# A graph network kernel on one core: the fourth sorted step of the third pass gathered by GpSimd instead of selected by TensorE

## The reference

```
h = relu(layernorm(x));                  # L0: two GCN convolutions
    h = relu(segment_sum((h @ W1)[src] * norm, dst) + b1)     # pass 1
    h = segment_sum((h @ W2)[src] * norm, dst) + b2           # pass 2
x = x + log_softmax(h)
h = relu(layernorm(x));                  # L1: GIN with edge attributes
    msg  = relu(h[src] + edge_attr @ We + be)                 # pass 3
    aggr = segment_sum(msg, dst)
    y = relu((h + aggr) @ W1 + b1) @ W2 + b2
x = x + relu(batchnorm(y) * gamma + beta)
```

## Time and profile before

| | us |
|---|---|
| median of 3 runs | 5606.34 |
| lowest, highest | 5599.08, 5607.18 |
| the profiled execution | 5616.2 |
| its span, first to last instruction | 5614.4 |
| TensorE busy, share of the span | 77% |
| GpSimd busy | 67% |
| VectorE busy | 66% |
| ScalarE busy | 23% |
| mean granted TensorE clock | 0.855 |

### The profile page before, as it was taken

The page is one execution under the profiler, slowest core; times in us unless marked ns, Lnnn a source line. Parts: engine busy times, 40 slices in busy tenths (PEclk is TensorE's granted clock), DMA queues, the critical chain, the costliest instruction groups (busy, mean ns, idle before and its releaser), DMA issues.

```text
span 5614.4 us, 116632 instructions
## 1 busy us (share of the span) xinstructions
PE 4328.9 (77%) x29893; PEld 3358.6 (60%) x29894; DVE 3689.5 (66%) x10748; ACT 1292.0 (23%) x4287; POOL 3768.6 (67%) x3554
## 2 busy tenths in 40 slices
PE   4566666666666666668999999996699999999995
PEld 4444444444444444456777777775577777777773
DVE  3466666665666666647888888886666666666662
ACT  5111111111111111142111111113433333332223
POOL 2377777777777777737777777775666665666663
PEclk6577787777778787859999999996899999999997
DMA  2122222222222222212222222223232322222224
GB/s 54 37 47 46 50 47 47 48 47 48 46 48 46 49 48 49 46 52 52 52 51 51 51 51 51 51 48 111 65 70 65 70 68 66 70 62 67 63 59 109
DMA packets 239972, 316.92 MB, mean 56 GB/s; under 512 B 69263, under 2 KB 175178, under 8 KB 239545
## 3 DMA queue, kind: packets, MB, share of 16 engines
q0 software_dynamic: 111232, 170.85, 15.6%
q1 hardware_dynamic: 128688, 145.48, 8.9%
HBM read 276.92 MB, written 39.15 MB: 56 GB/s over the span
## 4 chain that ended last, share of the span: by engine, by line
PE 60%; DVE 13%; POOL 11%; issue 10%; DVEq 2%; ACT 2%; DMA 1%; POOLq 0%; ACTq 0%; SPq 0%
PE psum L1222 26%; PE psum L1142 15%; POOL rows_g L658 11%; PE psum L1165 7%; PE psum L1129 3%; DVE x_tab L1662 2%; PE psum L1086 2%; PE psum L1150 2%; PE psum L1154 1%; DVE x_tab L1657 1%; DVEq L432 1%; PE psum L1214 1%; PE psum L1289 1%; DMA rows_g<-table,idx 1%; DVE rows_g L1619 1%
## 5 line engine op out<-in xcount | busy, mean ns | idle before, releaser
L658 POOL DMA_INDIRECT rows_g<-table,idx x3476 | 3605.6, 1037 | 1547.3 <-issue 1011.3
L1222 PE MATMUL psum<-x_tab 125*128 x8512 | 1148.9, 289 | 83.9 <-issue 46.2
L1142 PE MATMUL psum<-hot,rows_g 128*96 128x128 f32 x7512 | 1077.4, 297 | 143.5 <-DMA rows_g<-table,idx 70.7
L1142 PEld LDWEIGHTS psum<-hot,rows_g 128*96 128x96 f32 x7512 | 980.8, 181 | 236.4 <-issue 145.8
L1222 PEld LDWEIGHTS psum<-x_tab 125*128 125x128 bf16 x8512 | 827.3, 97 | 393.9 <-issue 135.0
L1165 PE MATMUL psum<-x_tab 128*104 128x512 bf16 x2432 | 614.5, 403 | 534.4 <-DVE x_tab L1662 526.3
L1582 DVE TENSOR_TENSOR acc<-acc,psum 96x128 f32 x1173 | 328.8, 280 | 962.9 <-PE psum L1142 945.2
L791 ACT ACTIVATE attr<-edge 128x12 f32 (+1 forms) x1173 | 243.5, 211 | 2806.3 <-PE psum L1142 2805.6
L1165 PEld LDWEIGHTS psum<-x_tab 128*104 128x104 bf16 x2432 | 303.1, 133 | 780.6 <-ACT x_tab L848 321.9
L1573 DVE TENSOR_SCALAR hot<-iota,attr 128x128 f32<-128x128 f32 x2504 | 686.4, 356 | 7.3 <-ACT acc L785 4.8
L1619 DVE TENSOR_REDUCE rows_g<-psum 128x384 f32<-128x1152 f32 x304 | 412.3, 1356 | 341.2 <-PE psum L1222 336.9
(11 more groups left out here) (255 smaller groups left out, 3692.3 us busy)
## 6 DMA issues: line engine op xcount, KB each, us to landing
rows_g<-table,idx POOLq DMA_INDIRECT x3476, 2.5
x_tab<-sorted_keys SPq DMA_DIRECT2D x304, 125.0 KB
x_more<-in_edge_attr_dram SPq DMA_DIRECT2D x238, 64.0 KB
sorted_attr<-x_tab SPq DMA_DIRECT2D x38, 384.0 KB
x_more<-sorted_attr SPq DMA_DIRECT2D x152, 96.0 KB
table<-x_tab SPq DMA_DIRECT2D x13, 840.0 KB
x_tab<-in_edge_attr_dram SPq DMA_DIRECT2D x38, 256.0 KB, 2.8
x_tab<-in_x_dram SPq DMA_DIRECT2D x2, 4200.0 KB
```

The source lines that it names most:

```text
L658: pool.indirect_dma_start(out=rows_g[u][0:np_, g * F:(g + 1) * F], out_offset=None, in_=table[p], in_offset=bass.IndirectOffsetOnAxis(ap=i ...
L1142: last = pe.matmul(ps_agg[t.b], rows_g[t.u][0:t.np_, g * F:(g + 1) * F], hot[t.h][0:t.np_, g, :], start=g == 0, stop=g == G - 1)
L1222: last = pe.matmul(ps_sel[c], mask[i % 2][j][:, c * P:(c + 1) * P], tab3[:, j:J - KB + 1 + j, :, :][:, bass.ds(w[c], 1), :, :].rearrange(" ...
```

## The change

In pass 3 the fourth sorted step of each iteration (step 9, `SEL[3]`, `MIX = 3`) is fetched by GpSimd like a gathered step: 4 indirect DMAs more per iteration. Its 40 selecting matmuls and its 10 masks go. Its edge term is still made by the four matmuls of L1214 from the sorted attributes, as a sum of three parts; `join_rows` adds up the parts into a scratch tile `terms` (which lies over mask tiles that nobody uses then), waits for itself and for the gather, and adds `terms` to the gathered rows. The key of that step is still loaded and converted. The mask semaphore is raised without masks.

Since the fourth select now has no masks, the transposes and products of the edge attributes that stood between them move: `EA_AT` now has two in stretch 1 (at masks 2 and 6), one in stretch 2 (at mask 4) and none in stretch 3. VectorE's edge terms follow (`TERMS`: 3, 2, 1, 0 per stretch instead of 3, 1, 1, 1), ScalarE's copies too (`COPY_AT`, `COPY_PAST`), and SyncE's loads of attributes are spread as 1, 1, 2, 2 over the stretches instead of 3, 2, 1, 0, with the first three ahead of the loop.

```diff
@@ Step
             def selected(self, p):
-                return p > 0 and self.sel
+                return p > 0 and self.sel and not self.mixed(p)
+            def mixed(self, p):
+                return p == 2 and self.sel and self.i == MIX
...
@@ SyncE, load_iter
-                    for k in ((0, 1, 2), (3, 4), (5,), ())[i]:
-                        t = Gather(it, k)
-                        load_ea(fast, t.gi, t.s, t.h, EP)
+                    for k in ((3,), (4,), (5, 6), (7, 8))[i]:
+                        t = Gather(it + k // NG, k % NG)
+                        load_ea(fast, t.gi, t.s, t.h, t.np_)
...
@@ ScalarE, gin_iter
+            COPY_AT, COPY_PAST = {0: (0,), 1: (1,), 2: (2,), 4: (3,), 5: (5,)}, {4: (4,)}
...
                     for k in SEGS[i]:
-                        if k in GAT:
-                            gin_copy(Gather(it, GAT.index(k) + LL))
+                        for g in COPY_AT.get(k, ()):
+                            gin_copy(Gather(it, g + LL))
                         relu_fast(Step(it, k))
+                        for g in COPY_PAST.get(k, ()):
+                            gin_copy(Gather(it, g + LL))
...
@@ TensorE, select
-                w = starts(it, i)
+                w = None if p == 2 and i == MIX else starts(it, i)
...
+                mixed = p == 2 and i == MIX
...
-                for j in range(KB):
+                for j in range(0 if mixed else KB):
...
-            EA_AT = ({2: 0, 5: 1, 8: 2}, {5: 3}, {5: 4}, {5: 5})
+            EA_AT = ({2: 0, 5: 1, 8: 2}, {2: 3, 6: 4}, {4: 5}, {})
...
@@ VectorE, make_masks
+                if p == 2 and i == MIX:
+                    dve.sem_inc(s_mask, KB)
+                    return
...
@@ VectorE, join_rows
+                if t.mixed(p):
+                    dve.tensor_reduce(terms.rearrange("e (c f) -> e c f", c=G), parts_of, AX.X, ALU.add).then_inc(s_terms, 1)
+                    dve.wait_ge(s_terms, t.it + 1)
+                    dve.wait_ge(fast_got[t.u], t.got(p))
+                    dve.tensor_tensor(rows_g[t.u], rows_g[t.u], terms, ALU.add).then_inc(s_row, 1)
...
@@ VectorE, fast_pass
+            TERMS = ((0, 1, 2), (3, 4), (5,), ())
...
-                        edge_terms = [Step(it, k) for k in SEGS[i] if p == 2 and k in GAT]
+                        edge_terms = [Step(it, GAT[g]) for g in TERMS[i] if p == 2]
```

More of the change, by code:

```diff
@@ L64, in build_gnn @@
     GAT, SEL = (0, 1, 2, 4, 6, 8), (3, 5, 7, 9)
+    MIX = 3
     SEGS = ((0, 1, 2), (3, 4), (5, 6), (7, 8, 9))
@@ L223, in build_gnn @@
         mask_t = [(at_free if k < 14 else at_low2 if k < 16 else at_top2).take(GE, BF16) for k in range(2 * KB)]
+        at_masks = at_free.tile[:, at_free.at - 4 * GE // 2:at_free.at]
         mask = [[t[0:PN, :] for t in mask_t[k * KB:(k + 1) * KB]] for k in range(2)]
+        terms = at_masks[:, 0:G * F]
         slow3 = mask_t[16][:, 0:3 * P].rearrange("p (t e) -> p t e", t=3)
@@ L318, in build_gnn @@
         s_sorted, s_edge = sem("group_sorted"), sem("sorted_edges_moved")
+        s_terms = sem("edge_terms_summed")
         s_bad, s_flag2 = sem("bad_summed"), sem("flag_again")
@@ L383, in got @@
             def got(self, p):
-                here = self.it + 1 if p == 0 or self.u in GAT else 1
+                here = self.it + 1 if p == 0 or self.u in GAT or p == 2 and self.u == SEL[MIX] else 1
                 return 16 * G * (USED[p][self.u] + here)
@@ L606, in _ @@
             load_key(2, 0, 1)
+            for k in range(EH):
+                t = Gather(0, k)
+                load_ea(fast, t.gi, t.s, t.h, EP)
             with sp.Fori(0, XI) as it:
@@ L611, in _ @@
             load_iter(LAST)
-            for k in range(REST):
+            for k in range(EH, REST):
                 t = Gather(LOOPS, k)
@@ L892, in relu_fast @@
             def relu_fast(t):
-                if t.selected(2):
+                if t.sel:
                     act.wait_ge(s_row, RS + t.pi + 2)
@@ L1213, in select @@
                     for c in range(G):
-                        pe.matmul(ps_sel[c], eaT3[i % 2][0:3 * KE, c * P:(c + 1) * P], we3[:, :, :].rearrange("q k f -> q (k f)"),
-                                  start=True, stop=False)
-                for j in range(KB):
+                        last = pe.matmul(ps_sel[c], eaT3[i % 2][0:3 * KE, c * P:(c + 1) * P], we3[:, :, :].rearrange("q k f -> q (k f)"),
+                                         start=True, stop=mixed)
+                for j in range(0 if mixed else KB):
                     if p == 2 and j in EA_AT[i]:
@@ L1618, in join_rows @@
                 dve.wait_ge(fast.staged, p * NS + t.s + 1)
-                dve.tensor_reduce(rows_g[t.u].rearrange("e (c f) -> e c f", c=G),
-                                  ps_sel4.rearrange("e c (k f) -> e c f k", k=3), AX.X, ALU.add).then_inc(s_row, 1)
+                parts_of = ps_sel4.rearrange("e c (k f) -> e c f k", k=3)
+                if t.mixed(p):
[3 more added lines that the diff above has]
+                    dve.tensor_tensor(rows_g[t.u], rows_g[t.u], terms, ALU.add).then_inc(s_row, 1)
+                else:
+                    dve.tensor_reduce(rows_g[t.u].rearrange("e (c f) -> e c f", c=G), parts_of, AX.X, ALU.add).then_inc(s_row, 1)
             def split(p):
```

## The result

The changed kernel takes 5650.8 us (median of 6 runs, 5636.8 to 5668.4), the kernel before 5605.3 in the same session (6 runs, 5598.2 to 5622.1): 1.0079 times as long, 95% interval 1.0057 to 1.0101. It is slower, by 45.6 us between the medians. The profiled execution took 5649.3 us, its span 5647.5; that is 33 us above the profiled execution before (5616.2).

The account below looks back on a forecast made before the run. TensorE, 93% busy, was taken as busiest, with VectorE less than 2 us behind it at the join of step 9. Work of -4 us plus +23 for the clock gave +19: 5635 profiled, 5625 against the median; range 5592 to 5660.

Parts of the forecast that it names:

- A: Whole kernel: -4 us from the work and +23 from the clock's fall, +19, 5625 against the median; chance 0.56.
- Stretch 3: Last stretch of a pass 3 iteration: aggregation of step 9 starts 1.55 us sooner, 1.69 gained in plain iterations.
- Stretch 1: Moved transpose and product add 0.76 us; in exponential iterations TensorE also waits 1.0 us for ScalarE's copy.
- Small things: Step 9's index tile delays stretch 0's first copy, 0.1 us over exponential iterations; SyncE's loads and the extra gathers cost nothing.
- rival B: Whole kernel: the clock holds, so only the -4 us sum counts, 5602; chance 0.22.
- The gap: TensorE in stretch 3: 3.2 us idle before step 9's aggregation, 0.9 ahead of that, every iteration, so the clock falls.
- The fall's price: TensorE at half clock for 3.4 us after the gap: 0 to 1.7 us lost, mean 0.62, +23 over 37 iterations.
- rival E: The clock costs its upper end, 1.7 us in each of 37 iterations, 63 less 4: 5665; chance 0.09.
- The fall's place: Three positions around step 9's aggregation and the first select, a third each: 0.9, 0.5 and 0.45 us lost.
- C: Stretch 3 gains 1.6 us, the clock holds, stretch 1 has no wait for the copy: 5578; chance 0.08.
- D: TensorE's work alone decides: 4.9 us less in each of 37 iterations, 181 us in all, 5425; chance 0.02.
- F: GpSimd becomes the bound in pass 3: at 1.5 us a gather an iteration takes 42 us, total 5710; chance 0.03.

Follow-up runs that it names:

- The third experiment: The changed kernel with stretch 1's two transposes issued ahead of masks 4 and 7 instead of 2 and 6: 5618.3 us, 1.0002 against the kernel before.

## Why the prediction was right, and where it was mis-sized

The forecast was A, slower by 19 us through the clock; it is slower by 46, in the range. The mechanism is shown, by the clock in the trace and by the run that holds the clock up. The size is not: 19 is less than half of 46, and that the time lies in the range is owed to the range's upper end, which put the clock's price at 1.55 us an iteration.

- **Stretch 3.** Forecast -1.55 us (plain -1.69), a join 5.7 us behind the one of step 7 with no wait. It is 5.44 us, no wait; the stretch is 1.8 shorter (10.2 to 8.4). Right, 0.2 low.
- **Stretch 1.** Forecast +0.76 for the pair and +1.0 for the copy, exponential iterations only. Measured 1.85 and 0.77; the wait is 0.83 us in 25 places. Right. The third experiment proves the wait apart.
- **Small things.** TensorE waits for no load, and the loop's turn is the same 1.7 to 2.3 us: nothing.
- **Sum with the clock held.** Forecast -4 us, +0.3 in an exponential iteration and -0.93 in a plain one; the run with dummy matmuls gives -8 (0.9984, 0.9970 to 0.9997), 0.0 and -1.2. Right: rival B's mechanism was the whole rest of the change, and only its condition, a clock that holds, failed.
- **The gap.** Forecast 3.2 us behind 0.9; measured 2.82 behind 0.99. Right.
- **The fall's price: the term that was mis-sized.** Forecast 0.62 us an iteration, 23 in all. Measured, against the run with dummy matmuls, 40.2 - 38.8 = 1.4 an iteration, and 48 us between the medians (53 by the ratios). What was wrong is the length. The slow piece was taken from the row of pass 2 as 3.4 us; it lasts 6.8 us here in 31 of 37 cases, and the granted clock over 4010 to 5390 is 0.92 and not 0.95 (6.8 at half in 41 is 0.92). The plain iterations have both lengths: stretch 0 is 12.8 us with the short piece and 14.2 to 14.3 with a long one that begins behind the aggregation too, against 12.4 with the clock held. So the short piece costs 0.4 us, near the 0.62 that I took, and the long one 1.9. In the exponential iterations about 2.0 us are lost between 4618.76 and 4625.29 (6.53 us from L1230 to the second transpose, against 4616.38 to 4620.92, 4.54 us, with the clock held, where 0.59 of waiting is in it). 6.8 us of half rate is 3.4 us of work, less the idle pieces in it, less what the waits absorb. The bound of 1.7 us (rival E, 5665) was the better guide, though it was made from the wrong length too.
- **The fall's place.** I put the fall at any of three positions with equal chance; no row of the kernel before shows that, and the mean of 0.9, 0.5 and 0.45 rests on it. In the plain iterations it does begin at different places, in the gap or behind the aggregation. In the exponential ones from 4142 us on it always begins in the last third of the aggregation of step 9, and nearly all of it lies on the 0.7 us of waiting behind and on the select. And what hits the aggregation is not lost in full (0.88 us): where the fall begins in the gap the aggregation takes 2.02 us and not 1.11, but the next L1230 starts 1.88 us behind its start, against 1.92 at full clock, since the 0.81 us of waiting at the loop's turn are gone.
- **Rivals.** C needed a stretch 1 without its wait: the wait was there. D: TensorE was busy 112 us less in the same 1380 us, and 181 us did not arrive. F, gathers too slow for 28 an iteration, did not happen where the change was judged (1002 ns each, GpSimd still waits 153 us in 34 iterations) but the gathers decide on the two other chips, there too without GpSimd as the limit: it idles half its time.
- **GpSimd's gap.** Forecast 7 to about 2 us. The longest waits of two iterations running are 2.44 and 3.69 us:

```profile
4631.63 0.94 POOL L669 DMA_INDIRECT rows_g<-table,idx  x1 [2.44 <-ACT idx L804]
...
4672.60 0.95 POOL L669 DMA_INDIRECT rows_g<-table,idx  x1 [3.69 <-ACT idx L804]
```

- **The Trainium skill.** By the rule of thumb of the Trainium skill's page "TensorE: Matmul & The Clock Gate", section "HAM oscillation — how this bites in real kernels", the clock would have held. The trace does not agree: with 2.82 us of idleness behind 0.99 us the clock fell in every iteration of the steady part. The measurement decides. The shutting out that the Trainium skill's page "SBUF — State Buffer", section "Who interferes with whom", led me to weigh cost nothing that can be seen: the add with both inputs in SBUF takes 0.56 us in all 34 cases, among gathers.

## What to carry to other kernels

Work that is taken off the busiest engine turns into a gap, and the gap has a price of its own: before counting the gain, find where the idleness will lie, and what the clock did behind pieces of that length in the same trace. Price a fall by the longest slow piece that can follow, not by one example, and by the work that stands behind the gap. A gap can have two causes of equal length (here a join and a PSUM tile's release), and an order that has room for one has to have room for both. Where the profile names no releaser of a wait, look for another engine that waits at the same time, and take only a cause that both wait for.

## What the runs showed of the hardware

- The slow piece can last 6.8 us at 1.2 GHz and come once an iteration at the same place; the iterations that alternated by 0.6 us before are then all 40.9 to 41.1 us. Where the iterations are shorter (the plain ones, 37.8 to 39.6 us) it lasts 3.4 or 6.8 us and its place changes.
- 21 dummy matmuls an iteration on zeros, 3.7 us of work in gaps, left no loss to be seen against the kernel before (0.9984) and gave 48 us back against the changed one.
- A kernel's time on another chip can be 1.24 to 1.26 times this chip's, and kernels with the four gathers and dummy matmuls that differ little from the one at -0.2% here are at +2.6 to +3.0% there.
- On those chips the semaphore of a product can be raised 12 us behind the product's recorded end; on the first chip it is 0.02 us at most.
